# A vision transformer layer on one core: attention scores as one fp32 product, and five splits of feed-forward weights done earlier

## The reference

```
h = concat(cls, layernorm(patches of x and of four shifted x) @ W + b)
n = layernorm(h);  q, k, v = n @ w.T + b               # 12 heads of 16
attn = softmax(q @ k.T / 4 + mask)                     # 37 x 37 for each image and head
h = h + (attn @ v) @ w_o.T + b_o
n = layernorm(h)
shared = silu(n @ ws_gate) * (n @ ws_up) @ ws_down     # 768 hidden
routed = two of eight experts with 192 hidden each, weighted by a router
h = h + alpha * shared + (1 - alpha) * routed
```

## Time and profile before

| | us |
|---|---|
| median of 3 runs | 176.16 (175.26 to 177.87) |
| profiled execution, its time | 175.75 |
| its span, first to last instruction | 173.9 |
| busy: PE / DVE / ACT / POOL | 139.3 / 120.5 / 91.0 / 42.1 |
| PE share of the span | 80% |

### The profile page before, as it was taken

The page is one execution under the profiler, slowest core; times in us unless marked ns, Lnnn a source line. Parts: engine busy times, 40 slices in busy tenths (PEclk is TensorE's granted clock), DMA queues, the critical chain, the costliest instruction groups (busy, mean ns, idle before and its releaser), DMA issues.

```text
span 173.9 us, 4192 instructions
## 1 busy us (share of the span) xinstructions
PE 139.3 (80%) x1673; PEld 111.0 (64%) x1673; DVE 120.5 (69%) x297; ACT 91.0 (52%) x198; POOL 42.1 (24%) x55
## 2 busy tenths in 40 slices
PE   0449999903399988769806999999899999999992
PEld 0218777802177977659704567888777778878782
DVE  6299854699899996994626479787596562542753
ACT  0588865941277924444265769445645534343340
POOL 0000010000000000000000035536846858668430
PEclk9999999995579999999995589999999999999998
DMA  5999997000000000004991000048300000000003
GB/s 160 386 368 364 327 263 305 0 0 0 0 0 0 4 4 4 4 4 135 402 410 53 0 0 4 0 113 331 123 0 4 0 0 4 4 0 0 4 0 105
DMA packets 7391, 16.89 MB, mean 97 GB/s; under 512 B 800, under 2 KB 3612, under 8 KB 7372
## 3 DMA queue, kind: packets, MB, share of 16 engines
q1 hardware_dynamic: 7012, 16.29, 26.9%
q10 hardware_dynamic: 360, 0.34, 0.7%
HBM read 16.15 MB, written 0.47 MB: 96 GB/s over the span
## 4 chain that ended last, share of the span: by engine, by line
PE 50%; DVE 24%; ACT 9%; issue 5%; DMA 5%; ACTq 3%; POOL 2%; SPq 1%; DVEq 0%; POOLq 0%
PE PS L566 19%; PE PS L594 10%; PE PS L403 5%; DMA stage<-in_f_d_dram 5%; DVE piece L959 3%; DVE xsq L1115 3%; DVE mx L1111 2%; PE PS L322 2%; PE PS L415 2%; DVE vhl L1256 2%; PE PS L343 2%; PE PS L345 2%; PE PS L346 2%; PE PS L309 2%; POOL vhl L850 1%
## 5 line engine op out<-in xcount | busy, mean ns | idle before, releaser
L859 POOL TENSOR_TENSOR kq<-vhl,kq 128x296 f16<-128x296 f32 x35 | 29.5, 843 | 96.3 <-ACT kq L811 96.1
L1256 DVE SCALAR_TENSOR_TENSOR vhl<-PS,vhl 128x296 f32<-128x296 f32 x36 | 16.8, 466 | 21.6 <-POOL vhl L850 12.1
L804 ACT ACTIVATE vhl<-PS 128x296 f32<-128x296 f32 x36 | 15.0, 416 | 27.5 <-PE PS L566 27.5
L811 ACT ACTIVATE kq<-vhl 128x296 f16<-128x296 f32 x36 | 16.0, 445 | 5.5 <-DVE vhl L1256 5.5
L375 PE MATMUL PS<-cst,hn 128*128 128x128 f32 x10 | 4.0, 401 | 13.4 <-DVE hn L1035 13.4
L850 POOL TENSOR_TENSOR vhl<-vhl,xs 128x296 f32<-128x296 f32 x14 | 12.6, 903 | 5.5 <-issue 4.8
L1245 DVE TENSOR_TENSOR vhl<-vhl,xs 64x296 f32<-64x296 f32 (+1 forms) x18 | 10.2, 566 | 2.8 <-ACT vhl L804 2.6
L566 PE MATMUL PS<-XAh,piece 128*128 128x296 f16 x48 | 11.1, 316 | 0.2 <-DVE vhl L1256 0.2
L375 PEld LDWEIGHTS PS<-cst,hn 128*128 128x128 f32 x10 | 2.0, 201 | 14.0 <-DVE hn L1035 14.0
L566 PE MATMUL PS<-XAh,slab 128*128 128x296 f16 x48 | 10.0, 290 | 0.9 <-DVE vhl L1256 0.9
L343 PE MATMUL PS<-whl,xhl 128*128 128x193 f16 (+1 forms) x40 | 10.5, 262 | 0.0
(11 more groups left out here) (215 smaller groups left out, 403.0 us busy)
## 6 DMA issues: line engine op xcount, KB each, us to landing
slab<-in_w_inner_dram SPq DMA_DIRECT2D x3, 960.0 KB, 9.5
xs<-gate_rows_dram SPq DMA_DIRECT2D x8, 296.0 KB, 5.8
xs<-in_x_inner_dram SPq DMA_DIRECT2D x3, 592.0 KB, 10.5
stage<-in_f_a_dram SPq DMA_DIRECT2D x2, 768.0 KB, 10.4
stage<-in_f_b_dram SPq DMA_DIRECT2D x2, 768.0 KB, 11.7
stage<-in_f_d_dram SPq DMA_DIRECT2D x2, 576.0 KB, 13.2
xhl<-in_f_a_dram SPq DMA_DIRECT2D x1, 768.0 KB, 8.4
xhl<-in_f_b_dram SPq DMA_DIRECT2D x1, 768.0 KB, 9.3
```

The costliest lines, as they stand in the source:

```text
L804: A(silu[:, i % 2, :], PS[:, 3 + 2 * (i % 2), 0:HALF], ACT.Silu, scale=1.0 / XW).then_inc(S["a_silu"], 1)
L811: A(ah[:, f % ABUF, half * HALF:(half + 1) * HALF], hf[:, i % 3, :], ACT.Copy).then_inc(S["a_ah"], 1)
L859: G.tensor_tensor(al[:, f % ABUF, cols], hf[:, i % 3, :], ah[:, f % ABUF, cols], ALU.subtract).then_inc(S["g_al"], 1)
L1256: V.scalar_tensor_tensor(out=hf[:, i % 3, :], in0=PS[:, 4 + 2 * (i % 2), 0:HALF], scalar=SH / XW, in1=src[:, i % 2, :], op0=ALU.mult, op1= ...
```

## The change

Scores become one fp32 matmul in place of two fp16 ones. ACT writes keys and queries in fp32 (`K32`, `Q32`), with the scale of 1/XW for the keys and 32/XW for the queries; as each head lies twice in the 32 rows, the exponential's scale is 1/256, as it was. `kq_low` and its twelve DVE instructions go. `ffn_high(0, 2)` and `(0, 3)` move between the `kq_high`, and `ffn_low(0, 0)` to `(0, 4)` move ahead of `differences(0)`, three of them into the time of the QKV products; `ffn_low(0, 5)` stands after `differences(1)`.

```
 scores(u):                                      # PE
-    for Q in (Q1, Q2):
-        for r in range(LANES):
-            mm(PS[.., 3 + r, ..], Q[rows, g, tok], KK[rows, g, tok], start=False, stop=(Q is Q2))
+    for r in range(LANES):
+        mm(PS[.., 3 + r, ..], Q32[rows, g, tok], K32[rows, g, tok], start=False, stop=True)
 QKV products, f >= 4:
-    pe.wait_ge(S["v_q2" if q4 else "v_kk"], ...)
+    pe.wait_ge(S["a_q" if q4 else "a_k"], ...)
 kq_high(f):                                     # ACT
-    A(Q1[..], PS[..], ACT.Copy, scale=SQ / XW)
-    A(kh[..], PS[..], ACT.Copy, scale=kscale)
+    A(Q32[..], PS[..], ACT.Copy, scale=QKS / XW)
+    A(K32[..], PS[..], ACT.Copy, scale=1.0 / XW)
 ACT's list:
     for f in range(3, 12):
         kq_high(f)
+        if f in (5, 8):
+            ffn_high(0, 2 + (f - 5) // 3)
+    ffn_high(0, 4)
+    ffn_high(0, 5)
     (ones into vv)
-    for q in range(2, 6):
-        ffn_high(0, q)
     exps(0)
 DVE's list:
-    attention_low(0..2, VC, AW), kq_low(0..2) between them
-    low_parts(0, (1, 2, 0), 1)
-    for f in range(3, 12): kq_low(f), and thrice after eight of them
+    attention_low(0..2, VC, AW)
+    ffn_low(0, 0)
+    thrice(0, 0); thrice(1, 0)
+    low_parts(0, (1, 2, 0), 1)
+    thrice(2, 0); thrice(3, 0); thrice(0..3, 1)
+    ffn_low(0, 1)
+    ffn_low(0, 2)
-    own_values(0..3)
-    ffn_low(0, 0)
-    ffn_low(0, 1)
+    own_values(0); own_values(1)
+    ffn_low(0, 3)
+    own_values(2); own_values(3)
+    ffn_low(0, 4)
     differences(0)
     ...
     in the loop over u, after differences(u + 1), own_values(7) and normalise(u - 1):
-        for q in ((), (2, 3, 4), (5,), ())[u]: ffn_low(0, q)
+        if u == 0: ffn_low(0, 5)
```

More of the change, by code:

```diff
@@ L54 @@
 PT_ = FT // PIECES
-SX, SW, SPIX, SPW, SK, SQ, SP_, SV, SCTX, SH = 64.0, 64.0, 16.0, 256.0, 16.0, 4.0, 256.0, 16.0, 16.0, 16.0
+SX, SW, SPIX, SPW, SK, SH, QKS = 64.0, 64.0, 16.0, 256.0, 16.0, 16.0, 32.0
 XW = SX * SW
 GATE_STEP = 6
+ABUF = 3
 CONSTS = 128 + 2 * CHUNKS + 1 + D + GROUPS + EXPERTS
@@ L149, in vit_kernel @@
         KFC = 2 * LANES * 4 * BLOCK
[L150 to L153, removed]
+        kq = sb("kq", [P, ABUF * NPAD])
+        K32 = xsq[:, KFC:KFC + GROUPS * N].rearrange("p (g n) -> p g n", g=GROUPS)
+        Q32 = kq[:, 0:GROUPS * N].rearrange("p (g n) -> p g n", g=GROUPS)
         vhl = sb("vhl", [P, IMAGES * LANES * VW])
@@ L190, in vit_kernel @@
         silu, sgate, hf = work[:, 0:2], work[:, 2:4], work[:, 4:7]
-        ABUF = 3
         ahlv = kq[:, 0:ABUF * NPAD].bitcast(F16).rearrange("p (k b n) -> p k b n", k=2, b=ABUF)
@@ L207, in vit_kernel @@
         names = """p_sq p_st p_bw p_main p_bias p_t p_k p_q p_v p_s p_pt p_av p_ct p_wo p_r p_gt p_gu p_dn p_end
-                   a_first a_xh a_xsq a_s0 a_ring a_bw a_sqr a_cs a_aw a_wh a_sqrt a_hi a_kh a_q1 a_vh a_exp a_pth a_chi a_e a_dup a_sig a_gt
+                   a_first a_xh a_xsq a_s0 a_ring a_bw a_sqr a_cs a_aw a_wh a_sqrt a_hi a_k a_q a_vh a_exp a_pth a_chi a_e a_dup a_sig a_gt
                    a_fw a_silu a_ah
-                   v_one v_ind v_pad v_aw0 v_jm v_jr v_xl v_fold v_wl v_awl v_mk v_stat v_h v_hn v_lo  v_kk v_q2 v_vm v_xr v_sg v_max v_sub
+                   v_one v_ind v_pad v_aw0 v_jm v_jr v_xl v_fold v_wl v_awl v_mk v_stat v_h v_hn v_lo  v_vm v_xr v_sg v_max v_sub
                    v_rows v_cn v_rd v_lg v_gate v_gx v_fw v_hf v_acc v_fin v_al v_bn
@@ L397, in _ @@
                     q4, g4, half4 = kq_product(f - 4)
-                    pe.wait_ge(S["v_q2" if q4 else "v_kk"], GROUPS * half4 + g4 + 1)
+                    pe.wait_ge(S["a_q" if q4 else "a_k"], GROUPS * half4 + g4 + 1)
                 cols = slice(half * HALF, (half + 1) * HALF)
@@ L430, in scores @@
                         for g in range(GROUPS):
-                            for Q in (Q1, Q2):
-                                for r in range(LANES):
[L433 to L437, removed]
+                            for r in range(LANES):
+                                rows = slice(32 * r, 32 * r + 32)
+                                col = pair * BLOCK + g * POSITIONS
+                                last = mm(PS[64 * bi:64 * bi + POSITIONS, 3 + r, col:col + POSITIONS],
+                                          Q32[rows, g, tok], K32[rows, g, tok], start=False, stop=True,
+                                          skip_group_check=True)
                 last.then_inc(S["p_s"], 1)
@@ L496, in _ @@
             pe.wait_ge(S["v_jr"], 2)
-            pe.wait_ge(S["v_kk"], 6)
-            pe.wait_ge(S["v_q2"], 6)
+            pe.wait_ge(S["a_k"], 6)
+            pe.wait_ge(S["a_q"], 6)
             scores(0)
@@ L735, in kq_high @@
                 if q:
-                    A(Q1[:, g, cols], PS[:, 3 + f % 4, 0:HALF], ACT.Copy, scale=SQ / XW).then_inc(S["a_q1"], 1)
+                    A(Q32[:, g, cols], PS[:, 3 + f % 4, 0:HALF], ACT.Copy, scale=QKS / XW).then_inc(S["a_q"], 1)
                 else:
-                    A(kh[:, g, cols], PS[:, 3 + f % 4, 0:HALF], ACT.Copy, scale=kscale).then_inc(S["a_kh"], 1)
+                    A(K32[:, g, cols], PS[:, 3 + f % 4, 0:HALF], ACT.Copy, scale=1.0 / XW).then_inc(S["a_k"], 1)
             root(0)
@@ L758, in exps @@
                     act.wait_ge(S["p_pt"], 2 * u - 2)
-                A(prob[:, u % 2], sdif[:, u % 2], ACT.Exp, scale=1.0 / (SK * SQ * 4)).then_inc(S["a_exp"], 1)
+                A(prob[:, u % 2], sdif[:, u % 2], ACT.Exp, scale=1.0 / (8 * QKS)).then_inc(S["a_exp"], 1)
             A(vv[:, :, :, GROUPS * HD:VW].rearrange("p b r o -> p (b r) o"),
@@ L1065, in _ @@
             variances(2)
[L1067 to L1078, removed]
             def thrice(i, half):
@@ L1092, in _ @@
             normed(0, (3, 4))
[L1093 to L1098, removed]
-            low_parts(0, (1, 2, 0), 1)
[L1100 to L1105, removed]
+            for k in range(3):
+                attention_low(k, VC, AW)
+            ffn_low(0, 0)
+            thrice(0, 0)
+            thrice(1, 0)
+            low_parts(0, (1, 2, 0), 1)
+            thrice(2, 0)
+            thrice(3, 0)
+            for k in range(4):
+                thrice(k, 1)
+            ffn_low(0, 1)
+            ffn_low(0, 2)
             def differences(u):
@@ L1138, in normalise @@
                                     [QROWS, 2, LANES, GROUPS, HD]), ALU.mult).then_inc(S["v_cn"], 2)
-            for i in range(4):
-                own_values(i)
-            ffn_low(0, 0)
-            ffn_low(0, 1)
+            own_values(0)
+            own_values(1)
+            ffn_low(0, 3)
+            own_values(2)
+            own_values(3)
+            ffn_low(0, 4)
             differences(0)
@@ L1153, in _ @@
                     normalise(u - 1)
-                for q in ((), (2, 3, 4), (5,), ())[u]:
-                    ffn_low(0, q)
+                if u == 0:
+                    ffn_low(0, 5)
             def add_attention(t):
```

## The result

The changed kernel takes **180.51 us** (median of 4, 179.85 to 180.91) against 176.13: ratio 1.0239, interval 1.0176 to 1.0301. It is 2.4% slower, where I had forecast 171.8.

A forecast was written before the change was run, and what follows sets the result against it. Bound: DVE splits on the attention path and piece 1's late fetch delaying the root. Gains of 4.68 us (0.7, 0.94, 3.06 by step) less 0.3 for fp32 scores took 176.16 to 171.8 us; range 169.9 to 174.1.

The forecast's parts named there:

- QKV products: QKV stretch: dropping kq_low frees 5.4 us of DVE for three splits, at no cost; differences(0) then starts 0.7 us earlier.
- fp32 scores: Four steps of scores: 0.15 us more each for 96 records; two steps on the path, 0.3 us lost.
- rival (c): Scores: row groups do not overlap in fp32, 2.5 us more a step, total 180.2 us; chance 0.05.
- rival (b): Scores: the matmul rate halves, 0.75 us more a step, total 173.4 us; chance 0.12.
- Piece 1: At the root: piece 1 lands early, so the root waits for DVE's variances, 86.7 instead of 91.40; 3.06 us gained.
- Behind the root: From the root to the end of the span: everything moves as one block, length unchanged at 82.5 us.
- I take it that PE's list meets the same place: In scores(3): PE's 0.88 us wait on "issue" recurs unchanged; differences(3) starts 1.64 us earlier, 0.94 us more gained.
- Rival (d): In scores(3): piece 1's DMAs slow PE's instruction packet, the gap grows, another 1.2 us lost, total 173.0 us; chance 0.14.
- rival (e): PE's gap in scores(3) vanishes (0.94 us more) or less idle time keeps the clock up (0.25 us); 170.6 us; chance 0.16.

The follow-up runs named there:

- e4: Kernel before, with three extra DMAs of piece 1's size (2.1 MB) into unused columns, issued when scores(2) is done: 179.82 us, ratio 1.0262.
- e7: Changed kernel with piece 1 issued after the fourth step of scores, and 15 or so implied PE waits left out: 171.33 us, ratio 0.9696.
- e6: Changed kernel with only the first of piece 1's three DMAs early, the other two after the fourth step of scores: 175.03 and 172.81 us, ratio 0.9848.
- e8: Kernel before, fp16 products and kq_low kept, with the splits moved and piece 1 issued after the fourth step of scores: 176.12 us, ratio 0.9994.
- e5: Kernel before with the fp32 scores alone, kq_low gone, all splits where they were: 176.93 us, ratio 1.0068.
- e1: Changed kernel with piece 1 late: SP waits for the fourth step of scores before issuing it: 172.27 us, ratio 0.9825.
- e10: The kernel of e1 measured again, on the same chip as the kernel of e7: 172.32 us, ratio 0.9751.

## Why the prediction was wrong

**Right, by step.** *QKV products:* PE's matmuls stay back to back and the splits fit; DVE even waited 2.01 us for the first values. The stretch came out 0.5 us longer and not 0.7 shorter, for a reason outside the change: PE's matmuls changed from 0.45 to 0.29 us at 51.6, while before they had done so at about 49.8. In the repeat of the late piece the clock rose at about 48.9, and the stretch took 15.0 us, under the forecast 15.2. *fp32 scores:* 96 records in 1.06 us instead of 0.93, 0.13 more, where 0.15 was taken; row groups do overlap in fp32, which ends rival (c), though the measured time is near its 180.2. That likeness is chance. The four passes of the Trainium skill ("FP8 and Floating Point Precision", TensorE Precision Notes), by which rival (b) would have come about, are not contradicted. They cost 0.13 us for a step instead of 0.75, so by my reading they mostly fitted into what a record waited for anyway; no run separates the two. *Piece 1:* landed in time, the root waits for DVE's variances and no longer for the DMA, 3.0 us gained of 3.06. *Behind the root:* 82.6 us against 82.5.

**Wrong: "I take it that PE's list meets the same place", with the gap at 0.88 us.** The step named the gap, and gave it the length that it had had with idle DMA engines, although the same change moved 2.1 MB into that time. It measured 3.98 us. Rival (d) said so with a chance of 0.14 and a price of 1.2 us; the true price of the gap alone is 3.5 us (3.98 against 0.45 with the late piece). Its picture was off too: it let the time from the packet to PE grow, 2.66 us before, and that was 2.27 here; what moved was the packet's start, by some 3.6 us.

**Missing: the clock.** In rival (e) I let the clock only gain, through less idle time before the second layer norm. That a gap could cost it, in the middle of a stretch that is PE from end to end, stood in no case. It is the larger part: 18.9 us against 13.2 from `differences(3)` to the variances, 5.7 us; with the transfer taken out and the idle time kept, 5.1.

The sum closes: from the late piece's execution (span 170.4) to the changed kernel's (179.1) are 8.7 us; `differences(2)` to `differences(3)` takes 8.10 instead of 4.52, 3.6 us, and the low clock 5.7, less 0.2 ahead of them and 0.3 behind the root. With both removed the change gives 172.3 us, and the forecast of 171.8, built from the same steps, is within its margin of about half a microsecond.

## What to carry to other kernels

Before a transfer is moved earlier, look at which packets of instructions move in its new place, and at every wait put down to "issue" there: such a gap may be hidden before and exposed after, and the transfer makes it longer. Some 4 us in which PE stands idle can cost more than they last, when long PE work follows (5.1 to 5.7 us more here). One wait on the queue that issues the DMA can be worth more than the whole edit: it took 7 to 8 us, where the edit was forecast to gain 4.4.

## What the runs showed of the hardware

- PE's instructions come in packets of 16 KB, and data transfers under way hold them back: with 2.1 MB issued ahead PE stood 3.98 us (3.02 in e4), with 0.77 MB 2.18, with none 0.45 to 0.88, or not at all (e7). The Trainium skill ("Runtime: NRT & Kernel Launch", Instruction fetch mechanics) has the blocks of 16 KiB and calls their cost mostly hidden; the trace agrees on the size, and here it was not hidden. The Trainium skill's rule for the queues ("DMA: Bandwidth & Descriptors", Queues, rings and completion order) is that an engine goes round its queues and changes after each packet; by it the block would have been served soon after it was asked for. It came some 3.6 us late, after about 1.5 of 2.16 MB, and in e4 some 2.5 us late, after 0.93. The measurement decides; whether the block or its request waited, no run here tells.
- Between the start of such a packet and the matmul that waited for it lay 2.2 to 2.7 us in nine traces, with and without data transfers beside it.
- After 4.0 to 4.2 us without matmuls the granted clock stayed at 1.2 GHz for 14 to 15 us more, though PE was busy nearly all of it (15.08 of 15.10 us in the changed kernel). In the profiled executions it also fell after shorter times without matmuls: 2.18 us (e6, there 2 us after PE had gone on), 2.13 us (e8) and 1.81 us (e5). After 1.59 us in the kernel before it stayed at 2.4 GHz.
- PE came out of the low clock of the QKV products at 51.7 us in the changed kernel, and at 52.1 and 48.9 us in two executions of one kernel text (e1, e10). From the first QKV matmul to `differences(0)` took 16.4, 16.6 and 15.0 us, so this alone moves the time by over one us.
